# One zero count of 5000 columns per row block in place of two, and the two halves freed together

## The reference, cut to what matters

```python
# layer 0: A is adj (5000 x 5000, zeros and ones), y one-hot (5000 x 16)
adj0 = A * (y @ y.T);  adj0 = adj0 / max(sum(abs(adj0), axis=1), 1e-12)
x = layernorm(x + 0.9 * (adj0 @ x) + 0.1 * h0)
# layer 1: T = 350
filt = tanh(A * A) * (A > 0);  new_adj = filt, the 350 largest of each row kept
h2 = tanh(x @ W_proj + b_proj)
x = layernorm(x + relu(new_adj @ (h2 @ W_gcn) + b_gcn))
```

## Time and profile before

| | |
|---|---|
| time, median of 3 runs | 497.94 us |
| profiled execution, its own time | 498.9 us |
| its span | 497.0 us |
| busy TensorE | 462.9 us, 93% |
| busy VectorE | 397.5 us, 80% |
| busy ScalarE | 276.8 us, 56% |
| mean granted TensorE clock | 0.993 of full speed |

### The profile page before, as it was taken

The page is one execution under the profiler, slowest core; times in us unless marked ns, Lnnn a source line. Parts: engine busy times, 40 slices in busy tenths (PEclk is TensorE's granted clock), DMA queues, the critical chain, the costliest instruction groups (busy, mean ns, idle before and its releaser), DMA issues.

```text
span 497.0 us, 15867 instructions
## 1 busy us (share of the span) xinstructions
PE 462.9 (93%) x5124; PEld 389.1 (78%) x5124; DVE 397.5 (80%) x1421; ACT 276.8 (56%) x496; POOL 192.5 (39%) x354
## 2 busy tenths in 40 slices
PE   3728999999999999999999999999999999999991
PEld 2314888888888888888888887888888888888881
DVE  4798799999999999999999996656666566556662
ACT  5456799999999999999999962660000000000000
POOL 3494254554444555554544553122212221122111
PEclk9999999999999999999999999999999999999997
DMA  7955799999999999999999900000000000000000
GB/s 184 401 190 197 296 410 410 415 402 401 402 406 383 409 391 390 412 389 416 387 400 403 405 12 2 2 18 16 11 16 16 16 11 16 16 16 16 11 17 18
DMA packets 29290, 108.44 MB, mean 218 GB/s; under 512 B 7753, under 2 KB 18018, under 8 KB 19266
## 3 DMA queue, kind: packets, MB, share of 16 engines
q1 hardware_dynamic: 29266, 108.14, 56.1%
HBM read 105.57 MB, written 2.56 MB: 218 GB/s over the span
## 4 chain that ended last, share of the span: by engine, by line
PE 83%; DVE 9%; issue 3%; POOL 3%; ACT 0%; POOLq 0%; DVEq 0%; ACTq 0%
PE acc L447 67%; PE words L435 7%; DVE a_bits L722 4%; PE proj_acc L501 3%; PE feat_acc L488 2%; PE acc L425 1%; PE xnt_acc L480 1%; POOL rstd L358 1%; DVE turned L709 1%; POOL pack L333 1%; PE proj_acc L425 1%; PE xnt_acc L425 1%; PE proj_acc L407 0%; DVE z_high L791 0%; DVE f_parts L644 0%
## 5 line engine op out<-in xcount | busy, mean ns | idle before, releaser
L447 PE MATMUL acc<-x_parts,turned 128*128 128x258 f16 (+1 forms) x1600 | 194.2, 275 | 2.0 <-DVE turned L709 1.7
L559 ACT ACTIVATE count_out<-a_rows,ones 128x2560 bf16<-128x2560 f32 (+1 forms) x80 | 189.7, 2371 | 5.8 <-issue 5.3
L447 PEld LDWEIGHTS acc<-x_parts,turned 128*128 128x128 fp8e4 (+1 forms) x1600 | 153.6, 98 | 30.4 <-issue 7.1
L447 PE MATMUL acc<-f_parts,turned 128*128 128x258 f16 (+1 forms) x1560 | 175.6, 273 | 0.0
L447 PEld LDWEIGHTS acc<-f_parts,turned 128*128 128x128 fp8e4 (+1 forms) x1560 | 151.1, 97 | 23.4 <-issue 0.2
L722 DVE TENSOR_SCALAR a_bits<-a_rows 128x2560 bf16<-128x2560 f32 (+1 forms) x80 | 123.0, 1540 | 2.9 <-PE words L435 1.0
L355 POOL TENSOR_TENSOR var_eps<-mean_var,consts 128x1 f32<-128x1 f32 (+1 forms) x80 | 18.6, 233 | 255.6 <-DVE mean_var L868 137.1
L709 DVE TENSOR_SCALAR turned<-a_words 128x320 uint16 (+1 forms) x305 | 67.3, 232 | 58.7 <-PE acc L447 58.7
L358 POOL TENSOR_TENSOR rstd<-var_eps,consts 128x1 f32<-128x1 f32 (+1 forms) x80 | 92.0, 1150 | 6.3
L709 DVE TENSOR_SCALAR turned<-same_class 128x320 uint16<-128x320 uint16 x313 | 79.4, 277 | 0.1
L435 PEld LDWEIGHTS words<-pack,a_bits 128*128 128x128 bf16 (+1 forms) x1600 | 51.2, 96 | 21.8 <-DVE a_bits L722 15.3
(11 more groups left out here) (104 smaller groups left out, 363.5 us busy)
## 6 DMA issues: line engine op xcount, KB each, us to landing
a_rows<-in_adj_dram SPq DMA_DIRECT2D x39, 1280.0 KB, 7.5
a_rows<-in_adj_dram SPq DMA_DIRECT2D x39, 1220.0 KB, 7.6
h_rows<-in_L_gnn_h_dram SPq DMA_DIRECT2D x39, 64.0 KB, 7.2
out_dram<-xn SPq DMA_DIRECT2D x39, 64.0 KB, 1.5
y_nat<-in_L_gnn_y_dram SPq DMA_DIRECT2D x1, 312.0 KB, 4.6
a_rows<-in_adj_dram SPq DMA_DIRECT2D x1, 80.0 KB
a_rows<-in_adj_dram SPq DMA_DIRECT2D x1, 76.2 KB
wp<-in_L_gnn_W_proj_dram SPq DMA_DIRECT2D x1, 64.0 KB, 9.9
```

What stands on the lines that cost most here:

```text
L447: mm = pe.matmul(acc[par][0:m, 0:PARTS], turned_at(n, par)[:, b, :].bitcast(F8)[:, 0:m], parts[:, b, :], start=first and b == blocks[0], s ...
L559: act.activation(count_out[0:m, 0:w], a_rows[par][h][0:m, 0:w], ACT.Relu, bias=ones[0:m, 0:1], scale=-HUGE, accum_out=col).then_inc(s_coun ...
```

## The change

The two tiles of a pair become one tile of 5120 columns with two views, the loads stay two, and ScalarE counts once per row block over 5000 columns, when both halves have landed and behind `xn_t`. `s_counted` now counts row blocks, so both halves' loads wait for the same count.

```diff
-        a_rows = [[sb(f"a_rows{p}{h}", [P, HB * P]) for h in range(2)] for p in range(2)]
+        a_full = [sb(f"a_rows{p}", [P, NB * P]) for p in range(2)]
+        a_rows = [[a_full[p][:, h * HB * P:(h + 1) * HB * P] for h in range(2)] for p in range(2)]
-        count_out = sb("count_out", [P, HB * P], BF16)
+        count_out = sb("count_out", [P, N], BF16)
-        zeros_in = sb("zeros_in", [P, 2 * NB])
+        zeros_in = sb("zeros_in", [P, NB])
@@ load_rows (SyncE)
                         sp.wait_ge(s_bits, t * 2 - 3 + h)
-                        sp.wait_ge(s_counted, t * 2 - 3 + h)
+                        sp.wait_ge(s_counted, t - 1)
@@ count_zeros (ScalarE)
-                act.wait_ge(s_rows[par][h], pair * 16 + 16)
-                w = HALF[h].stop - HALF[h].start
-                col = zeros_in[0:m, bass.ds(t * 2 + h, 1)]
-                act.wait_ge(s_counted, t * 2 + h)
-                act.activation(count_out[0:m, 0:w], a_rows[par][h][0:m, 0:w], ACT.Relu,
+                for h in range(2):
+                    act.wait_ge(s_rows[par][h], pair * 16 + 16)
+                act.wait_ge(s_counted, t)
+                act.activation(count_out[0:m, :], a_full[par][0:m, 0:N], ACT.Relu,
                                bias=ones[0:m, 0:1], scale=-HUGE,
-                               accum_out=col).then_inc(s_counted, 1)
+                               accum_out=zeros_in[0:m, bass.ds(t, 1)]).then_inc(s_counted, 1)
@@ step (ScalarE), behind a_words and h2_t
-                if valid(t):
-                    count_zeros(t, par, pair, 0, rows_of(t))
                 if valid(t - 5):
...
                     act.activation(xn_t[:, 0:m5], xnt_acc[:, 0:m5], ACT.Copy).then_inc(s_xnt_sb, 1)
                 if valid(t):
-                    count_zeros(t, par, pair, 1, rows_of(t))
+                    count_zeros(t, par, pair, rows_of(t))
@@ check_sums (VectorE, once, in the second phase)
-                dve.wait_ge(s_counted, 2 * NB)
-                zeros_in_2 = zeros_in[:, :].rearrange("p (b h) -> p b h", h=2)
-                done(dve.tensor_tensor(chk[:, :], zeros_in_2[:, :, 0], zeros_in_2[:, :, 1], ALU.add))
-                done(dve.tensor_scalar(need[:, :], chk[:, :], -1.0, float(N), ALU.mult, ALU.add))
+                dve.wait_ge(s_counted, NB)
+                done(dve.tensor_scalar(need[:, :], zeros_in[:, :], -1.0, float(N), ALU.mult, ALU.add))
```

More of the change, by code:

```diff
@@ L52, in packed_path @@
     PARTS = 2 * F + 2
-    CHECKS = 11
+    CHECKS = 10
     EARLY = NB - 4
@@ L550, in high_parts, with count_zeros @@
                 gram_copies(GRAM[0])
-            def count_zeros(t, par, pair, h, m):
-                act.wait_ge(s_rows[par][h], pair * 16 + 16)
-                w = HALF[h].stop - HALF[h].start
-                col = zeros_in[0:m, bass.ds(t * 2 + h, 1)]
-                act.wait_ge(s_counted, t * 2 + h)
-                act.activation(count_out[0:m, 0:w], a_rows[par][h][0:m, 0:w], ACT.Relu,
+            def count_zeros(t, par, pair, m):
+                for h in range(2):
+                    act.wait_ge(s_rows[par][h], pair * 16 + 16)
+                act.wait_ge(s_counted, t)
+                act.activation(count_out[0:m, :], a_full[par][0:m, 0:N], ACT.Relu,
                                bias=ones[0:m, 0:1], scale=-HUGE,
-                               accum_out=col).then_inc(s_counted, 1)
+                               accum_out=zeros_in[0:m, bass.ds(t, 1)]).then_inc(s_counted, 1)
             def measure(parts, sums, t, n):
@@ L617, in _ @@
             dve.memset(g_words[:, :, LAST * WORDS:NB * WORDS], 0)
-            dve.memset(zeros_in[:, :], N / 2)
+            dve.memset(zeros_in[:, :], N)
             for a in (degree, x_sums, f_sums):
```

## The result

The changed kernel takes 531.08 us, the median of 4 runs (527.98 to 532.55), against 497.89 before. The ratio is 1.0664 (95% interval 1.0611 to 1.0716). The direction was forecast, the size was not: 33.2 us more, where 12 were forecast and 521 was the upper end. The profiled execution took 532.55 us, its span 530.7. Ratios leave out executions over 1.5% above the fastest of the same kernel; beside after_three_quarter_loads and short_count_small_loads that leaves only the shortest of the kernel before, one of which took 489.65 us, so these two ratios are larger than the medians make them (510.3 and 497.4 against 497.2).

A forecast was written before the change was run, and what follows sets the result against it. TensorE's chain was taken to bound the kernel at 6.58 us a step; loops through ScalarE's count and the loads make it 6.88, (6.88 - 6.58) x 34 = 10.2, plus 1 for edges: 11.2 us. Forecast 510.0 us, range 503.5 to 521.

The forecast's parts named there:

- ScalarE's order: The whole count behind `xn_t` delays `a_words`, so VectorE's `same_class` waits; a loop of 13.66 us for two steps, 6.83 each.
- the prediction's own sign of being wrong: In the changed kernel's profile, VectorE showing no idle time ahead of `same_class`; about 0.4 us a step was forecast.
- sign that the loads decide: VectorE idle ahead of `a_bits` and ScalarE ahead of the count, both released by DMA.
- the rows near idle: Profile rows where half 0's load had nothing queued ahead, 5.7 us, or an idle queue at issue, half 1 behind, 6.2.
- L: Time of half 0's load from issue to landing, taken as 6.0 us; the rows ran from 5.7 to 7.4.
- first load loop: Count end, issue, both halves landed, next count in the same buffer: 7.77 us + L for two steps, 6.89 a step.
- half 1 3.0 us behind half 0: Half 1's load lands about 3.0 us after half 0's, from 1.25 MB at 412 GB/s.
- loop B: The first load loop as read from half 1's issue: both halves landed, count, next issue; 15.42 us for two steps.
- The rival that came true: The loads set the pace: at a landing of 7.4 us, 7.59 us a step and 533 us; chance 0.15, for all over 517.
- The edges and the clock: First-phase start and end add 1 us, bounds 0 and 3; no change of TensorE's clock counted for 0.3 us waiting a step.

The follow-up runs named there:

- after_three_quarter_loads: The changed kernel with loads of 1920 columns a half from step 3 on; 510.3 us, ratio to the kernel before 1.034.
- short_count_small_loads: The changed kernel counting 2560 of the 5000 columns, check on degrees left out, with loads of 640 columns a half from step 3 on; 497.4 us, ratio 1.006.
- behind_together: The kernel before with both counts, still two operations, moved behind `xn_t` and both halves' loads waiting for the second count; 532.0 us, ratio 1.069.

## Why the prediction was wrong

*Right: which part of the order closes a loop, and nearly its size.* ScalarE's order was forecast to make 6.83 us a step; without the loads it makes 6.97 to 7.0, so over the 6.58 it costs 0.39 and not 0.25, 13.7 us in all. The terms that were off are the steps from one engine to the next: `a_words` to `same_class` 0.16 (0.03 was set), unpack to multiply 0.24 (0.05 was set, and the row's 0.21 put aside since TensorE was projecting then; it projects again), `xn_t` to count 0.27 (0.18), the copy 0.16 (0.25). The count took 4.46 (4.42). The Trainium skill ("ScalarE: Activation LUTs", What ACT_TABLE_LOAD costs) gave 4.45 us for it, and the trace agrees within 0.01. ScalarE idles 23.9 / 22 = 1.09 us a step ahead of `xn_t` in the run with small loads, where 1.1 was forecast. VectorE's wait of 8.1 / 21 = 0.39 us was forecast as 0.4, but it stands one instruction earlier, ahead of `f_rest`, which waits for `f_parts`; `same_class` comes right behind it. In the changed kernel itself little of this is left, 3.8 us ahead of `f_rest` and 0.2 ahead of `same_class` in 150 us. Next to no idle time there was the prediction's own sign of being wrong; the casts' 23.6 us for DMA are its sign that the loads decide. The row is of the run with small loads:

```profile
L596 ACT ACTIVATE xn_t<-xnt_acc 128x128 f32<-128x128 f32 x22 | 6.1, 278 | 23.9 <-PE xnt_acc L484 23.9
```

*Wrong: "In the new order the block before is nearly through when a load is issued, so I go by the rows near idle and take L = 6.0."* This is the step that failed. L was 6.9 in the median, and in the loops read above 7.5. With 6.9 the prediction's own first load loop gives (7.77 + 6.9) / 2 = 7.33 a step and 498 + 0.75 x 34 + 1 = 525 us. The block before was not nearly through: the load issued at 161.47 still had half 1 under way at 172, 2 us after the next issue at 169.83. The rows near idle, 5.7 and 6.2, were of loads issued on idle DMA engines (0 GB/s from 55.0 to 55.4); the changed kernel shows 5.5 for such a load, half 1 close behind it. The row that had the block before in it was the steady 7.4, and it was discounted as "much of it queue". The queue was the kernel's own, and stayed.

*Right: half 1 3.0 us behind half 0.* In the medians it is 0.65 + 9.5 - 6.9 = 3.25. The load issued at 161.47 landed after 7.5 and its half 1 after 0.65 + 9.8 = 10.45, 2.95 behind. With L = 7.5 the prediction's first load loop gives 7.64 a step, where loop B as read is 7.71: the loop was right, and L was the term that was off.

*Missed: loop D.* The cast of half 0 also leads straight to the packing, the transpose and `xn_t` of its own step, L + 7.45 us for two steps. At L = 6.0 it would have been 6.7, hidden under the 6.83 and of no consequence for the forecast; at 6.9 it is 7.2, at 7.5 it is 7.5, and with the wait for half 1 inside it, it is as long as B. In behind_together it is what is left.

*The rival that came true* was priced at 533 us with L = 7.4, with a chance of 0.15. The price is right because both halves had landed after 7.4 + 3.0 = 10.4 us in it, and 10.15 in the median, 10.65 in the loop, were measured; that half 0 landed after 6.9 and not 7.4, and that loop D lies beside it, it didn't have. So the price holds in part by luck. What spoke for it was in the rows: the loads were to decide from L = 5.9 on, and the landing times shown ran from 5.7 to 7.4.

*The load's own time.* The Trainium skill ("DMA: Bandwidth & Descriptors", Anatomy of one DMA) has a fixed 2.0 us and 436 GB/s, for the GpSimd path and not SyncE's; the estimate from it is 5.0 us for half 0 and 2.8 for 0.33 MB. No landing read here is under 5.5 for half 0; the small loads of 0.33 MB took 2.9 to 3.0.

*The edges and the clock* were small, as forecast: the 34 steps make 33 of the 33.2 us. In the changed kernel's 100 to 125 us TensorE was granted 0.86 of full speed in the mean, which takes at most 0.14 x 25 = 3.5 us off it. How much of that lies on a path, no run here shows; beside the first runs, executions of the kernel before with a mean granted clock of 0.96 took no longer (495.97 to 498.06 us) than those with 0.99 (496.25 to 497.92).

## What to carry to other kernels

When two pieces of a double buffer are freed by one operation, the load's issue moves to the last reader. Put it into every loop through that buffer, with the landing time of the traffic that the kernel really has, not of a load on an idle queue: ask whether the block before is still moving at the issue. Where loops lie within a few tenths of each other, forecast from the longest landing seen. Before merging two operations to save their fixed cost, ask what stood between them and whether a cover goes: here the engine saved 0.4 us a step that nobody waited for, and what had been counted in the shadow of a wait now stood in front of what others needed.

## What the runs showed of the hardware

- A load of 1.31 MB (1280 KB) took 5.5 to 6.2 us from issue to landing on idle DMA engines, with or without a second of 1.25 MB issued 0.65 us behind it. With the block before still moving it took 6.7 to 7.9 us (medians of the runs with full pairs). The pair was down 8.5 us after the first issue in the first case (0.65 + 7.8), and after 9.9 to 11 in the second; one transfer of both (2500 KB) took 9.1.
- TensorE's clock was granted in full in the kernel before until its last stage, though TensorE was hardly idle; in the changed kernel it was at the lower level, 1.2 GHz, from 105 to 111 us (0.50), behind 102 to 105 us, in which TensorE was busy 0.5 us of 3. The changed kernel with small loads, with TensorE busy 23.2 of 25 us in 150 to 175, shows 1.00 there. The run with three quarters of the loads was granted 0.50 from 20 to 45 us and was no slower than the one with small loads.
